# The opening of a fused MetaFormer kernel: corner experts placed ahead of the gates, attention with a second value buffer, and half of the weight splitting moved to POOL

## The chip, the cores and the metric

The kernel runs on one core of a Trainium2 chip. The metric is the device time of one execution in microseconds. Three runs of the kernel before gave 2888.99, 2886.65 and 2889.01 us, median 2888.99 us. The execution whose profile is read here took 2888.1 us, of which 2886.3 us are the span that the profile shows.

## The reference

The input is 16 images of 16x16 positions with 128 channels (4096 tokens). Two layers follow, each with residual sums:

```
x = x + attention(ln_c(x))          # k, v softmax over positions; 64x64 descriptor per image; Wr
t = t + experts(ln_t(t))            # softmax gate, top 2 of 8 experts, each 128 -> 512 gelu -> 128
x = x + grouped_conv(ln_c(x))       # 3x3, 8 groups
t = t + ode(ln_t(t))                # y0 = t[:, 0]; 255 Runge-Kutta steps of a tanh MLP 128-512-512-128
```

The last term is a chain: the solution at position s is step s of an ordinary differential equation whose start is position 0 of every image. Everything is float32; the kernel splits weights and activations of the large products into two float16 halves (high and low) and adds three products.

## The kernel before

**The two parts.** The kernel is a short opening and a long chain. The chain is 255 Runge-Kutta steps; all other work on the 4096 tokens (experts, convolution) is placed beside its steps. The chain needs y0, the final normalised value of position 0 of each image, and that needs the attention of all tokens and then experts and convolution for the four corner positions only. So the opening computes: transposes of x, a first layer norm, attention for four pairs of 512-token tiles, a second layer norm with the gate's logits, the gates, the eight experts for 64 corner tokens, two small norms and the corner of the convolution. Then step 0 starts.

**Order.** All orders are written out by hand, engine by engine; engines meet through counting semaphores. The opening is straight-line code apart from the attention rounds, which are a loop (`Fori`) of three and one written out.

**Attention round i** (`attention_round`, lines 553 to 577 for TensorE, 973 to 985 for ACT, 1159 to 1181 for DVE). TensorE transposes the exponentials of pair i (L557), projects pair i+1 (L549 for keys and queries, L551 for values), forms the descriptors (L565), the output (L571) and the projection Wr (L576), and then waits for the residual of the round. ACT copies TK, copies keys and queries of i+1, copies the output OT, copies the values of i+1 (one buffer V, so only after L571 has read it) and takes the exponentials of i+1 (`exps`, L968 and L970). DVE takes the maxima of the keys of i+1 (L1156), scales the descriptors (L1166), makes the high halves of the fused weights RHU (L1170), takes the maxima of the values, adds the residual to X (L1184), and makes low halves of weights.

**Weight halves.** POOL makes the high halves (L396): four quarters, each of W1 and W2 (1024 columns), RH2 (512), RH3 (128) and CKH (288). DVE makes the low halves of the same, and of the three fused weights (3 x 512 columns), eight instructions a round (`low_halves`, L1189 and L1192). In the last round they stand ahead of the residual.

**Norm, gates, corner experts.** `layer_norm(1)` runs TensorE means (L510) and variances (L516), ACT square, logarithm and exponential, DVE subtraction and product (L1132, L1142), with the gate's logits (L598) beside it. The gates are a chain of 22 DVE instructions (`link`, L1253 to L1275), with one exponential on ACT. TensorE then turns the gates (`turn(0)`, L606), spreads the corner scores (L615), and runs the experts (L625 to L637) with gelu on ACT (L1016) and the split of its result on DVE (L1285, L1287). POOL waits for the gates (`g_ss`) and splits the normalised tokens N into NH (L402) and NL (L405). DVE's small constants (`identities`, `constant`) stand ahead of and between the experts. L1291 closes the experts; the two small norms (`layer_norm` of 64 and 16 columns, L1304 to L1306) give y0 (`rk_y`).

**Step 0** waits on TensorE for the injected base (`rk_ai`), for NL (`n_lo`) and for the gates copied out (`g_sc`). POOL's `base_low(0)` is wanted by TensorE ahead of the last layer of step 0, NH and NL first by the experts beside step 1. SP writes the gates to HBM (L370) and reads them back row by row (L373) into SC, which lies in the memory of the fused weights' source.

## Time and profile before

| what | us |
|---|---|
| three runs, median (lowest, highest) | 2888.99 (2886.65, 2889.01) |
| profiled execution, its own time | 2888.1 |
| its span | 2886.3 |
| TensorE busy, share of the span | 2805.1, 97% |
| DVE busy | 2359.0, 82% |
| ACT busy | 1549.3, 54% |
| POOL busy | 726.9, 25% |

The busy shares are those of the whole span, and 94% of the span is the chain of steps. What is changed lies in the first 168.3 us, so the views to read are the table of busy time by stretch and the timeline of the opening. In a timeline row the first number is the start in us from the span's start, the second the time from start to end of the group, then engine, line, operation, output and inputs with their shape, the count, and in brackets the idle time of that engine before it with what ended it.

### The profile page before, as it was taken

What the parts mean: (1) busy time and instruction counts of PE and PEld (TensorE: products, weight loads), DVE (VectorE), ACT (ScalarE), POOL (GpSimd) and SP (SyncE); (2) the same over time, 40 slices, a digit from 0 to 9 for tenths busy, and PEclk for the clock granted to TensorE, in tenths of its full rate; (3) what the DMA queues carried; (4) which work ended last, traced back from release to release, by engine and by line L of the source; (5) the groups of instructions that cost most, each with busy time, mean ns of one, the idle gap of its engine ahead of it and who ended that gap; (6) DMA issues with size and microseconds to landing.
All of it is one profiled execution on the core that took longest, in us unless ns stands there. A gap on an engine that the chain in (4) does not pass through costs nothing.

```text
span 2886.3 us, 207890 instructions
## 1 busy us (share of the span) xinstructions
PE 2805.1 (97%) x81958; PEld 2402.4 (83%) x81958; DVE 2359.0 (82%) x13272; ACT 1549.3 (54%) x10124; POOL 726.9 (25%) x1346
## 2 busy tenths in 40 slices
PE   7789999999999999999999999999999999999999
PEld 3478888888888888888888887888889999999998
DVE  5778888888888888888888887888888888888887
ACT  6455555555555555555554444444445555555555
POOL 5222332332332332332332000111112222222222
PEclk9789999999999999999999999999999999999999
DMA  3000000000000000000000000000000000000000
GB/s 118 0 12 11 13 12 11 13 12 11 14 12 11 14 12 11 14 12 11 14 11 8 1 0 1 0 0 0 0 17 0 0 0 0 0 0 0 0 0 15
DMA packets 21982, 28.21 MB, mean 10 GB/s; under 512 B 4384, under 2 KB 12896, under 8 KB 21544
## 3 DMA queue, kind: packets, MB, share of 16 engines
q1 hardware_dynamic: 21928, 27.48, 3.1%
q8 instruction: 36, 0.59, 0.1%
q14 instruction: 18, 0.15, 0.0%
HBM read 25.24 MB, written 2.23 MB: 10 GB/s over the span
## 4 chain that ended last, share of the span: by engine, by line
PE 93%; DVE 3%; ACT 2%; issue 1%; DMA 0%; SPq 0%; DVEq 0%; ACTq 0%; POOLq 0%; POOL 0%
PE PSUM L681 22%; PE PSUM L687 21%; PE PSUM L888 17%; PE PSUM L742 12%; PE PSUM L672 5%; PE PSUM L884 4%; PE PSUM L779 1%; DVE PSUM L1395 1%; PE PSUM L844 1%; PE PSUM L849 1%; PE PSUM L708 1%; ACT HA L1072 1%; PE PSUM L712 1%; PE PSUM L749 1%; PE PSUM L510 1%
## 5 line engine op out<-in xcount | busy, mean ns | idle before, releaser
L1395 DVE TENSOR_REDUCE PSUM<-PSUM 128x32 f32<-128x64 f32 x2912 | 624.9, 232 | 96.8 <-PE PSUM L687 51.1
L681 PEld LDWEIGHTS PSUM<-HA,RL 128*128 128x128 f16 x11648 | 396.3, 96 | 205.8 <-ACT HA L1072 196.4
L1073 ACT ACTIVATE PSUM<-PSUM 128x32 f32<-128x32 f32 x2912 | 562.1, 194 | 0.0
L1072 ACT ACTIVATE HA<-PSUM 128x32 f16<-128x32 f32 x1456 | 287.6, 198 | 469.2 <-DVE PSUM L1395 469.1
L1072 ACT ACTIVATE HB<-PSUM 128x32 f16<-128x32 f32 x1456 | 287.9, 199 | 466.0 <-DVE PSUM L1395 466.0
L681 PE MATMUL PSUM<-HA,RL 128*128 128x16 f16 x11648 | 512.1, 170 | 15.3 <-ACT HA L1072 7.6
L681 PE MATMUL PSUM<-HB,RLU 128*128 128x16 f16 x11648 | 511.0, 170 | 3.6
L422 POOL TENSOR_TENSOR G<-G 128x512 f16<-128x512 f32 x256 | 296.6, 1159 | 682.9 <-ACT G L1045 682.9
L687 PE MATMUL PSUM<-HA,RH 128*128 128x32 f16 x11648 | 466.0, 177 | 0.0
L687 PE MATMUL PSUM<-HB,RHU 128*128 128x32 f16 x11648 | 464.8, 177 | 0.0
L681 PEld LDWEIGHTS PSUM<-HB,RLU 128*128 128x128 f16 x11648 | 393.6, 96 | 46.7 <-ACT HB L1072 1.9
L687 PEld LDWEIGHTS PSUM<-HA,RH 128*128 128x128 f16 x11648 | 403.8, 96 | 0.0
L687 PEld LDWEIGHTS PSUM<-HB,RHU 128*128 128x128 f16 x11648 | 402.8, 96 | 0.0
L1405 DVE TENSOR_TENSOR HB<-PSUM,HB 128x32 f16<-128x32 f32 x1456 | 279.9, 192 | 123.0 <-ACT PSUM L1073 114.7
L1405 DVE TENSOR_TENSOR HA<-PSUM,HA 128x32 f16<-128x32 f32 x1456 | 279.9, 192 | 101.1 <-ACT PSUM L1073 86.8
L1045 ACT ACTIVATE G<-PSUM,B1E 128x512 f16<-128x512 f32 (+1 forms) x512 | 353.7, 691 | 0.0
L888 PE MATMUL PSUM<-HB,RLU 128*128 128x32 f16 (+1 forms) x4672 | 338.4, 176 | 0.0
L888 PE MATMUL PSUM<-HA,RL 128*128 128x32 f16 (+1 forms) x4672 | 330.8, 176 | 0.3 <-ACT HA L1107 0.3
L1114 ACT ACTIVATE PSUM<-PSUM 128x16 f32<-128x16 f32 (+1 forms) x1749 | 318.9, 184 | 0.0
L1497 DVE TENSOR_REDUCE PSUM<-PSUM 128x16 f32<-128x32 f32 x1166 | 218.6, 200 | 85.0 <-PE PSUM L888 70.1
L888 PEld LDWEIGHTS PSUM<-HA,RL 128*128 128x128 f16 x4672 | 260.1, 96 | 11.5 <-ACT HA L1107 0.4
L888 PEld LDWEIGHTS PSUM<-HB,RLU 128*128 128x128 f16 x4672 | 260.2, 96 | 11.2
(307 smaller groups left out, 6686.7 us busy)
## 6 DMA issues: line engine op xcount, KB each, us to landing
G<-scores SPq DMA_DIRECT2D x64, 256.0 KB, 3.1
N<-in_x SPq DMA_DIRECT2D x8, 256.0 KB, 4.7
NHL<-in_w SPq DMA_DIRECT2D x1, 2048.0 KB, 10.1
STF<-in_w SPq DMA_DIRECT2D x1, 2048.0 KB, 14.6
out<-W2HL SPq DMA_DIRECT2D x8, 256.0 KB, 2.4
G<-in_r SPq DMA_DIRECT2D x1, 1024.0 KB, 5.3
R1K<-in_r SPq DMA_DIRECT2D x1, 256.0 KB, 2.9
R3F<-in_r SPq DMA_DIRECT2D x1, 256.0 KB, 5.4
```

The costliest lines, as they stand in the source:

```text
L422: g.tensor_tensor(GL[:, m], GF[:, m % 2], GH[:, m], ALU.subtract).then_inc(mo_lo, 1)
L681: mm(out[m // 2][:, 2 * B * (m % 2):2 * B * (m % 2) + B], lo[:, k, m], src[:, k, 0], start=False, stop=False)
L687: t = mm(out[m // 2][:, bass.ts(m % 2, 2 * B)], hi[:, k, m], src[:, k], start=False, stop=(stop and m % 2 == 1 and k == 3))
L742: t = mm(out[:, :], w, v, start=start, stop=stop)
L888: t = mm(repeated(1 - lay, m, B, copies), (lo if kind == "L" else hi)[:, k, m], half, start=False, stop=ends)
L1045: A(GF[:, m % 2] if full else GH[:, m], PS[5 + m % 2][:, :], ACT.Gelu, bias=B1E[:, m:m + 1], scale=1.0 / SCALE_M).then_inc(mo_f if full el ...
L1072: A(hi[:, 2 * h:2 * h + 2, 0], src, ACT.Tanh, scale=1.0 / scale).then_inc(rk_hi, 1)
L1073: A(full, src, ACT.Tanh, scale=1.0 / scale).then_inc(rk_f, 1)
L1114: A(SPLIT_FULL[lay][:, sl], SPLIT_SUM[lay][:, sl], ACT.Tanh, scale=1.0 / scale).then_inc(sp_f[g], 1)
L1395: v.tensor_reduce(bank[:, SUM:SUM + 2 * B].rearrange("p (m b) -> p m b", m=2), bank[:, 0:4 * B].rearrange("p (m c b) -> p m b c", m=2, c=2 ...
L1405: TT(hi[:, sl, 1], full, hi[:, sl, 0], ALU.subtract).then_inc(rk_lo, 1)
L1497: v.tensor_reduce(SPLIT_SUM[lay][:, ms[0]:ms[-1] + 1], PAIRED[lay][g - 1].rearrange("p (m c b) -> p m b c", m=len(ms), c=2), AX.X, ALU.add ...
```

## The change

It changes the order of work in the opening; nothing is left out. The attention rounds are written out for all four pairs. V becomes two buffers, the second in free memory of the norm. The projection of pair i+1 stands ahead of the transposes of pair i, and ACT copies the values of i+1 directly behind the keys. DVE takes the maxima of i+1 ahead of RHU, keeps the low halves of W1 and W2 only, and puts the residual between them. The low halves of the Runge-Kutta, convolution and fused weights (six per quarter) are made by POOL behind the high halves, each with two instructions: a scaled copy in float32 (new buffer SCALED) and a subtraction. Step 0 waits for these 24 (`r_lo`). The corner tokens are split and the experts start directly behind the logits; the gates are made in five parts between the first experts, `turn(0)` stands behind the up-products of the sixth expert and the spreading of scores behind those of the eighth. ACT makes NH, one tile beside each expert. POOL makes NL only behind y0 (`rk_y`), beside step 0; TensorE waits for it ahead of step 1. The constants move into the waits of the small norms.

```diff
-        V = sb("V", [DIM, 2, TILE])
+        V = (sb("V", [DIM, 2, TILE])[:, :, :], SQ4[0:DIM, 2:4])
...
# SP
             sp.wait_ge(w_lo, 4)
+            sp.wait_ge(r_lo, 24)
             sp.dma_start(SC, scores[0:1, :].partition_broadcast(128)).then_inc(sc_in, 16)
...
# POOL
             for q in range(4):
-                for hi, _lo, src, scale in quarter(q):
+                for n, (hi, _lo, src, scale) in enumerate(quarter(q)):
                     t = g.tensor_scalar(hi, src, scale, None, ALU.mult)
-                t.then_inc(w_hi, 1)
+                    if n == 1 or n == 4:
+                        t.then_inc(w_hi, 1)
+            gp.wait_ge(w_hi, 8)
+            for q in range(4):
+                for n, (hi, lo, src, scale) in enumerate(quarter(q)[2:] + fused_quarter(q)):
+                    if n == 3:
+                        gp.wait_ge(u_hi, q + 1)
+                    scaled = SCALED[:, 0:math.prod(src.shape[1:])].rearrange("p (q n) -> p q n", q=1)
+                    g.tensor_scalar(scaled, src, scale, None, ALU.mult).then_inc(r_mul, 1)
+                    gp.wait_ge(r_mul, 6 * q + n + 1)
+                    t = g.tensor_tensor(lo, scaled, hi, ALU.subtract)
+                    t.then_inc(r_lo, 1)
+                    gp.wait_ge(r_lo, 6 * q + n + 1)
             gp.wait_ge(ln_out, 2 * NT)
             gp.wait_ge(w_lo, 4)
-            gp.wait_ge(g_ss, 1)
-            g.tensor_copy(NH, N[:, :]).then_inc(n_hi, 1)
-            gp.wait_ge(n_hi, 1)
+            gp.wait_ge(pm_lo, NE)
+            gp.wait_ge(n_hi, NT)
+            gp.wait_ge(rk_y, 1)
             for t in range(NT):
-                r = g.tensor_tensor(NL[:, bass.ts(t, TILE)], N[:, bass.ts(t, TILE)], NH[:, bass.ts(t, TILE)], ALU.subtract)
-            r.then_inc(n_lo, 1)
+                g.tensor_tensor(NL[:, bass.ts(t, TILE)], N[:, bass.ts(t, TILE)], NH[:, bass.ts(t, TILE)], ALU.subtract).then_inc(n_lo, 1)
...
# TensorE
             def project(i):
+                if i:
+                    pe.wait_ge(at_kq, 2 * i)
...
+                if i:
+                    pe.wait_ge(at_v, 2 * i)
...
-            def attention_round(i, nxt=True):
+            def attention_round(i):
+                if i + 1 < PAIRS:
+                    project(i + 1)
                 for par in range(2):
                     pe.wait_ge(at_exp, 2 * i + par + 1)
...
-                if nxt:
-                    project(i + 1)
                 for par in range(2):
+                    if i:
+                        pe.wait_ge(at_x, 2 * i - 1 + par)
                     pe.wait_ge(at_tk, 2 * i + par + 1)
...
-                pe.wait_ge(at_x, 2 * i + 2)
...
-            pe.wait_ge(g_ss, 1)
-            turn(0)
-            pe.wait_ge(g_stc, 4)
-            for e in range(NE):
-                t = mm(PS[3][:, bass.ts(e, PT)], SELE[:, e], STC[:, :], start=True, stop=True)
-            t.then_inc(pm_s, 1)
+            pe.wait_ge(g_v, 2)
...
                 t.then_inc(pm_h, 1)
+                if e == NE - 3:
+                    pe.wait_ge(g_ss, 1)
+                    turn(0)
+                if e == NE - 1:
+                    pe.wait_ge(g_stc, 4)
+                    for n in range(NE):
+                        t = mm(PS[3][:, bass.ts(n, PT)], SELE[:, n], STC[:, :], start=True, stop=True)
+                    t.then_inc(pm_s, 1)
                 if e:
                     down(e - 1)
...
-            pe.wait_ge(n_lo, 1)
             pe.wait_ge(g_sc, 8)
+            pe.wait_ge(r_lo, 24)
             step(0, True)
+            pe.wait_ge(n_lo, NT)
             moe_round(step, expert, -1, late=False)
...
# ACT
-                if nxt:
+                if i + 1 < PAIRS:
                     copy_kq(i + 1)
+                    copy_v(i + 1)
                 for par in range(2):
                     act.wait_ge(at_o, 2 * i + par + 1)
                     nc.scalar.copy(OT[:, par], PA[par][0:DIM, :]).then_inc(at_ot, 1)
-                if nxt:
-                    copy_v(i + 1)
+                if i + 1 < PAIRS:
                     exps(i + 1)
...
                 t.then_inc(pm_g, 1)
+                nc.scalar.copy(NH[:, bass.ts(e, TILE)], N[:, bass.ts(e, TILE)]).then_inc(n_hi, 1)
+                if e == NE - 2:
+                    corner_scores()
...
             act.wait_ge(w_lo, 4)
+            act.wait_ge(r_lo, 24)
             step(0, True)
...
# DVE
-            def attention_round(i, nxt=True):
+            def attention_round(i):
+                reciprocals(i)
...
                     t.then_inc(at_gds, 1)
+                if i + 1 < PAIRS:
+                    maxima(i + 1, 0)
+                    maxima(i + 1, 1)
                 for hi, lo, src, scale in fused_quarter(i):
                     t = TS(hi, src, scale, None, ALU.mult)
                 t.then_inc(u_hi, 1)
+                dve.wait_ge(w_hi, 2 * i + 1)
+                low_half(quarter(i)[0])
+                residual(i)
+                low_half(quarter(i)[1]).then_inc(w_lo, 1)
...
             link(TT(GA[:, :, :], LOGITS, wide(0), ALU.subtract))
             v.tensor_copy(corners(PNH[:, :]), corner(N[:, :])).then_inc(pm_n, 1)
             dve.wait_ge(pm_n, 1)
             TT(corners(PNL[:, :]), corner(N[:, :]), corners(PNH[:, :]), ALU.subtract).then_inc(pm_n, 1)
-            identities()
+            biases()
...
+            gates(0)
             for e in range(NE):
...
                 TT(PGL[:, e % 2], PGF[:, e % 2], PGH[:, e % 2], ALU.subtract).then_inc(pm_lo, 1)
-                if 3 <= e < 7:
-                    constant(e - 3)
+                gates(e + 1)
+            identities()
...
                 TT(D[:, 0, 0:width], src[:, :], PA[0][:, 0:width], ALU.subtract).then_inc(ln_dev, 1)
+                constant(2 * n)
```

The five parts of the gates hold 5, 4, 4, 4 and 3 of the 20 instructions from L1256 to L1275, in their old order.

## Rows read from the trace of the kernel before

**Rows 1.** Stretch, length; busy us (count) of PE, PEld, DVE, ACT, POOL; PE clock; DMA
```profile
38.20:98.80 60.60, 44.53 (x169) 23.45 (x169) 45.34 (x96) 30.49 (x84) 41.82 (x19) 0.79 0.00 0
98.80:123.60 24.80, 24.40 (x104) 15.18 (x104) 11.13 (x18) 13.99 (x24) 0.00 (x0) 0.91 0.00 1
123.60:155.90 32.30, 15.34 (x227) 12.44 (x228) 25.49 (x60) 12.84 (x43) 13.05 (x9) 0.63 0.01 1
...
143.41:144.69 1.28, 1.27 (x24) 1.27 (x24) 1.25 (x2) 0.00 (x0) 1.28 (x2) 0.50 0.06 13
...
168.30:2886.30 2718.00, 2685.99 (x81342) 2332.24 (x81342) 2258.51 (x13063) 1461.08 (x9914) 665.03 (x1311) 0.99 0.02 7
```

**Rows 2.** Timeline, TensorE: the matmul groups of an attention round, and the last round's start
```profile
29.75 1.96 PE L549 MATMUL PSUM<-N,WKQ 128*128 128x512 f32 x4
...
61.66 1.09 PE L565 MATMUL PSUM<-SQ 128*64 128x64 f32 x16
...
62.92 1.99 PE L571 MATMUL PSUM<-V,GD 64*128 64x256 f32 x8 [0.17 <-DVE GD L1166]
...
64.75 1.95 PE L576 MATMUL PSUM<-D,WR 64*128 64x512 f32 x4
...
84.94 0.66 PE L557 MATMUL PSUM<-ID,D 128*128 128x128 f32 x4 [2.33 <-ACT V L970]
```

**Rows 3.** Timeline, ACT: first exponential of one pair, and the TK copy behind the last
```profile
66.90 0.51 ACT L968 ACTIVATE D<-D,NM 64x256 f32<-64x256 f32 x1 [0.22 <-DVE NM L1156]
...
70.85 0.56 ACT L977 COPY SQ<-PSUM 128x512 f32<-128x512 f32 x1
```

**Rows 4.** Timeline, DVE: one attention round
```profile
63.25 1.08 DVE L1170 TENSOR_SCALAR RHU<-G  x3
...
66.14 1.27 DVE L1156 TENSOR_REDUCE NM<-V 64x2 f32<-64x512 f32 x2 [1.81 <-ACT V L960]
...
67.34 1.39 DVE L1184 SCALAR_TENSOR_TENSOR X<-PSUM,BR,X 128x512 f32 x2
...
68.65 1.21 DVE L1189 SCALAR_TENSOR_TENSOR W1HL<-NHL,W1HL  x1
```

**Rows 5.** Timeline, TensorE: the means of the first and of the second layer norm
```profile
12.33 3.70 PE L510 MATMUL PSUM<-X,ONES 128*128 128x512 f32 x8 [0.76 <-ACT X L947]
...
98.78 6.02 PE L510 MATMUL PSUM<-X,ONES 128*128 128x512 f32 x8 [2.95 <-DVE X L1184]
```

**Rows 6.** Timeline, POOL: high halves, the last of them, and the eight NL subtractions
```profile
38.17 1.49 POOL L396 TENSOR_SCALAR RH<-G 128x512 f16<-128x512 f32 x1
...
68.41 8.20 POOL L396 TENSOR_SCALAR W2HL<-STF 128x1024 f16<-128x1024 f32 x1
...
78.72 1.79 POOL L396 TENSOR_SCALAR CKH<-CK 128x288 f16<-128x288 f32 x1
...
137.44 9.39 POOL L405 TENSOR_TENSOR NHL<-N,NHL 128x512 f16<-128x512 f32 x8
```

**Rows 7.** Timeline, DVE: instructions beside a busy POOL, and a cast beside an idle one
```profile
38.20 0.59 DVE L1198 TENSOR_TENSOR RP<-SE 64x2 f32<-64x2 f32 x1 [3.21 <-ACT V L970]
...
143.28 1.24 DVE L1285 CAST SQ<-D 128x256 f16<-128x256 f32 x1
...
150.01 0.29 DVE L1285 CAST SQ<-D 128x256 f16<-128x256 f32 x1 [0.33 <-PE PSUM L627]
```

**Rows 8.** Timeline, DVE, TensorE and ACT: first and last gate, turn, spreading of scores, gelu
```profile
125.02 0.42 DVE L1256 TENSOR_REDUCE GR<-GP 128x32 f32<-128x256 f32 x1 [0.56 <-ACT GP L998]
...
133.11 0.42 DVE L1275 TENSOR_TENSOR GP<-GP,GR 128x256 f32<-128x256 f32 x1
...
133.59 3.58 PE L606 MATMUL PSUM<-ID,GP 128*8 128x128 f32 x16 [10.04 <-DVE GP L1275]
...
137.41 2.08 PE L615 MATMUL PSUM<-STC,SELE 8*128 8x64 f32 x16 [0.25 <-ACT STC L1005]
...
150.64 0.93 ACT L1016 ACTIVATE D<-PSUM,B 128x64 f32<-128x64 f32 x4 [0.72 <-PE PSUM L637]
```

More of the change, by code:

```diff
@@ L17 @@
+import math
 from contextlib import ExitStack
@@ L219, in build @@
         ck_zero, consts, w_hi, u_hi, w_lo = (sem(k) for k in ("ck_zero", "consts", "w_hi", "u_hi", "w_lo"))
+        r_mul, r_lo = sem("r_mul"), sem("r_lo")
         x_tr, x_c = sem("x_tr"), sem("x_c")
@@ L583, in _ @@
             pe.wait_ge(w13_out, MC)
-            with pe.Fori(0, PAIRS - 1) as i:
+            for i in range(PAIRS):
                 attention_round(i)
-            attention_round(PAIRS - 1, False)
+            pe.wait_ge(at_x, NT)
             def logits(place):
@@ L992, in _ @@
             exps(0)
-            with act.Fori(0, PAIRS - 1) as i:
+            for i in range(PAIRS):
                 attention_round(i)
-            attention_round(PAIRS - 1, False)
             layer_norm(1, 1)
@@ L1001, in turned, with corner_scores @@
                 nc.scalar.copy(dst, PS[4 + k][0:NE, :].rearrange("e (b n) -> e b n", b=4)).then_inc(g_sc, 1)
[L1003 to L1008 removed]
+            def corner_scores():
+                for k in range(4):
+                    act.wait_ge(g_st, k + 1)
+                    nc.scalar.copy(STC[:, bass.ts(k, PT // 4)].rearrange("e (b y x) -> e b y x", b=4, y=2),
+                                   PS[4 + k][0:NE, :].rearrange("e (b y x) -> e b y x", b=4, x=HW)[:, :, 0:2, 0:2]).then_inc(g_stc, 1)
             nc.scalar.preload_act_table_set("gelu_and_others")
+            act.wait_ge(w_lo, 4)
             for e in range(NE):
@@ L1017, in _ @@
                 t.then_inc(pm_g, 1)
+                nc.scalar.copy(NH[:, bass.ts(e, TILE)], N[:, bass.ts(e, TILE)]).then_inc(n_hi, 1)
+                if e == NE - 2:
+                    corner_scores()
+            for k in range(4):
+                turned(k, 0)
             nc.scalar.preload_act_table_set("natural_log_exp_and_others")
@@ L1025, in _ @@
                 A(SD[:, 0, 0:width], SD[:, 0, 0:width], ACT.Exp, scale=-0.5).then_inc(ln_sd, 1)
-            for k in range(4):
-                act.wait_ge(g_st, 4 + k + 1)
-                turned(k, 1)
+                if n == 0:
+                    for k in range(4):
+                        act.wait_ge(g_st, 4 + k + 1)
+                        turned(k, 1)
             nc.scalar.preload_act_table_set("gelu_and_others")
@@ L1171, in attention_round @@
                 t.then_inc(u_hi, 1)
-                if nxt:
-                    maxima(i + 1, 1)
-                    residual(i)
-                    low_halves(i)
-                    reciprocals(i + 1)
-                else:
-                    low_halves(i)
-                    residual(i)
+                dve.wait_ge(w_hi, 2 * i + 1)
+                low_half(quarter(i)[0])
+                residual(i)
+                low_half(quarter(i)[1]).then_inc(w_lo, 1)
             def residual(i):
@@ L1184, in residual, with low_half @@
                     STT(X[:, tile(i, par)], PB[par][:, :], BR[:, :], X[:, tile(i, par)], ALU.add, ALU.add).then_inc(at_x, 1)
-            def low_halves(i):
-                dve.wait_ge(w_hi, i + 1)
-                for hi, lo, src, scale in quarter(i):
-                    STT(lo, src, scale, hi, ALU.mult, ALU.subtract)
-                dve.wait_ge(u_hi, i + 1)
-                for hi, lo, src, scale in fused_quarter(i):
-                    t = STT(lo, src, scale, hi, ALU.mult, ALU.subtract)
-                t.then_inc(w_lo, 1)
+            def low_half(half):
+                hi, lo, src, scale = half
+                return STT(lo, src, scale, hi, ALU.mult, ALU.subtract)
             def reciprocals(i):
@@ L1204, in _ @@
             maxima(0, 1)
-            reciprocals(0)
             dve.wait_ge(w13_out, MC)
-            with dve.Fori(0, PAIRS - 1) as i:
+            for i in range(PAIRS):
                 attention_round(i)
-            attention_round(PAIRS - 1, False)
             dve.wait_ge(at_x, NT)
```

77 lines of the change are left out of this document (39 added, 38 removed).

## The prediction

> **What bounds the kernel now.** I read the busy time by stretch first [rows 1], then the timeline of the opening engine by engine. The chain of 255 steps begins at 168.3 us and takes 2718.0 us, 10.7 a step; the change touches nothing in it, so I price the 168.3 us ahead of it. Four stretches matter: attention (38.2 to 98.8), second norm with logits (to 123.6), gates and corner experts (to 155.9), small norms (12.4 us, to 168.3). In attention no engine is busy for more than 45.3 of 60.6 us, and TensorE's clock is granted at 0.79: engines wait for each other in turn. In the third stretch TensorE is busy for 15.3 of 32.3 us, and its first turn stands behind 10.04 us of idling on the last gate [rows 8]. Only the norm is full (TensorE 24.4 of 24.8 us). So there is room in two stretches, and little in the others.
>
> **Attention.** The last round's transposes start at 84.94 [rows 2], the first at 38.2: 15.6 us a round. The change takes the projection from behind the transposes, the values' copy and maxima from behind the output, and six low halves a round from DVE. What is left for TensorE at full clock is two transposes (0.66 each), two projections (1.96 each), 1.09, 1.99 and 1.95: 10.3 us [rows 2]. DVE keeps RHU 1.08, four maxima 2.54, residual 1.39 and two low halves 2.42: 7.4 [rows 4], which leaves 2.9 for the small scalings and for waits on POOL. So TensorE sets the round at 10.3, and as it then hardly idles I take the full clock; that is the floor, 10.3 / 0.79 = 13.0 the ceiling. The last interval holds no projection; there ACT decides: transposes 0.7, six copies of about 0.56, the two key copies and two value copies among them longer, and half of the exponentials make about 8.
>
> The first transposes wait for exponentials and now also for a projection. A pair's exponentials take 70.85 - 66.90 = 3.95 [rows 3] and begin once W13 is copied out, at 38.2 less half of that: 36.2. Only then can the projection run ahead (3.9), so the first transposes move from 38.2 to 40.1, a loss of 1.9. Then 10.3 + 10.3 + 8 lead to 68.7. From there the last round took 98.78 - 84.94 = 13.8 [rows 2, 5]. Now it is: second half of the exponentials 2.0, transposes 0.7, TK copy 0.6, half of the products 0.5, scaling 0.5, half of the output 1.0, OT copy 0.6, half of Wr 1.0, residual 1.4, and 0.4 for POOL; RHU and one low half lie beside the others. That is 8.7: the norm starts at 77.4, not 98.78, **21.4 gained**.
>
> The added waits cost nothing by this. The projection waits for copies made a round earlier, the products for the last residual. DVE's `w_hi` waits for POOL's W1 and W2 of the round's quarter; behind it stand the residual and, through it, the next products. POOL ends all quarters at 80.51 now, with 5.2 us lost on each of two W2 instructions that stood still (8.20, against 3.0 at 1.49 for 512 columns) [rows 6], so without such stalls W2 of the last quarter is there by about 72, and is wanted at about 74. If it is not, each us late is a us lost.
>
> **Norm.** Its means took 6.02 against 3.70 in the first norm [rows 5]: they followed 2.95 us of idling and the clock was low; that idling goes, so 2.3 less. But POOL is now busy beside it. A cast beside POOL's subtractions took 1.24, beside an idle POOL 0.29: it waited 0.95, where one such subtraction takes 9.39 / 8 = 1.17 [rows 6, 7]. Eight multiplies with two SBUF inputs may each wait that long, 0 to 7.6 us; TensorE's pace hides most, I take 1.0. **1.3 gained**; the logits end at 100.9.
>
> **Gates and experts.** Now 32.3 us [rows 1]. After: 0.9 for two links and 1.2 for corner halves and biases (estimates from 0.42 and 0.29); five gates; then for each of four experts a cast of 0.29 and a subtraction of 0.42 with 15 gates between them. The 20 gates ran from 125.02 to 133.53 [rows 8], 0.43 each: 0.9 + 1.2 + 8.5 + 2.8 = 13.4 to the last gate. ACT's table load, gelu (0.93) and NH copies (about 0.56, as the TK copy [rows 3]) lie beside these, since 1.5 an expert on ACT is under 2.4 on DVE. POOL's locks add 0 to 24 (some 25 exposed instructions at 0.95); POOL's scalings and subtractions leave the lock free about half the time and DVE fills part of it, I take 4.0. Behind the last gate stand the turn 3.58, two products of 0.64 (24 matmuls in 1.27 at half clock [rows 1]), gelu and NH 1.5, four score copies 0.6, spreading 2.08, two products of 0.64: 10.3 at half clock, 6.2 at full; I take 8.2 [rows 8]. Sum 25.6: **6.7 gained**; L1291 starts at 126.5. Constants and the second turn's copies go into waits of the small norms; one that sticks out costs up to 0.6; I take 0.4, so 12.8 there. The first injection comes at 139.3, **29.0 earlier**.
>
> **POOL.** Its high halves end between 66.9 (80.51 less two stalls of 5.2 and three RHU runs of 1.08) and 77.4 (that plus 3.5 of contending DVE work in each of three rounds); I take 72. Then each quarter has 2464 columns to scale and to subtract: 7.2 at 1.49 per 512, and 5.6 at 1.17 [rows 6]. A scaled copy to float32 is not in the trace: bounds 0.9 per 512 and 2.0, the nearest row kept. With 48 hand-overs of 0.1 (estimate) that is 56 us. DVE's contending work in that stretch adds 0 to 16 (half of the norm's 11.13, gates, casts); half is 8. The last low half lands at 136, 3 us ahead of the injection, so the new wait of TensorE, ACT and SP costs nothing; if it lands later, all three wait. NL (9.39) now follows y0 beside step 0, where DVE reads mostly PSUM; behind it on POOL stand the copy of y0 and `base_low(0)`, wanted 7/8 into a step of 10.7, at 9.4: 0 to 1.0, I take 0.
>
> **Sum.** 21.4 + 1.3 + 6.7 - 0.4 = 29.0 off the profiled execution's own 2888.1, which is 0.9 under the median of the runs: **2859 us**.
>
> **A rule against it.** The POOL instruction at 38.17 ran until 39.66; DVE's two-operand instruction beside it ended at 38.79 [rows 6, 7]: the wait was shorter than the instruction. The Trainium skill, "SBUF — State Buffer", section "Who interferes with whom", says that a DVE instruction with two SBUF inputs or in a two-port mode and a POOL instruction exclude each other for the whole instruction; the trace agrees that they do, not on how long. By it the sum would be that of rival 3.
>
> **Rivals.** (1) *POOL ends last* (0.17). High halves at 77.4 and 16 us of blocking put the last low half at 149; step 0 waits with all else ready: 19 gained, 2869. For it: W2 stood still twice [rows 6]. Against: DVE's runs are shorter now. (2) *The half clock stays in attention* (0.12). Two rounds of 13.0, one of 9 and slow means lose 8.7: 2868. For it: 0.79 now [rows 1]. Against: TensorE's work now fills the exponentials' time. (3) *Exclusion for the whole instruction* (0.13). POOL is busy until about 130; from 103 on one DVE instruction passes per POOL instruction of 1.2, 22 of 25 in that time, so the last gate comes near 132 rather than 118, and 2 are lost in the norm: 13 gained, 2875. (4) *Better* (0.12): no lock waits (5.4) and full clock behind the gates (2.0): 2852. (5) *Slower* (0.04): POOL's pairs of scaling and subtraction starve. 24 pairs from 72 on: at (168.3 - 72) / 24 = 4.0 us a pair step 0 starts as late as now, while the rows give 56 / 24 = 2.3; at 4.5 it starts at 180: 2900. (6) *Nothing is moved in the end* (0.03): what attention gives comes back as the wait for `r_lo`, 2888.
>
> **How the numbers follow.** The forecast has 0.39. The range takes in rivals 1 to 4 up to their outer parts and leaves out (5) and (6): 2848 to 2876. A measurement of this kernel can tell about 0.2%, 5.8 us, from no change: faster 0.93 (forecast and rivals 1 to 4), same 0.03, slower 0.04.
>
> **What would show it.** Right: transposes of successive rounds 10 to 11 us apart, then 8, at a granted clock near 1; the norm starting near 77; the last gate near 118 with casts of the first experts between the gates; the last low half on POOL a few us ahead of the injection; step 0 and all later steps as long as before. Wrong: TensorE idle ahead of step 0 with POOL as its releaser (1); a clock under 0.85 in attention (2); gates or casts that take 1 us or more (3); `w_hi` as a releaser of DVE ahead of a residual.

## The result, and the profile after

Four executions of the changed kernel took 2866.97, 2864.96, 2862.34 and 2871.75 us, median 2865.97; the kernel before took 2888.61 beside them (four executions). The ratio is 0.9925, 95% interval 0.9913 to 0.9938: 0.75% faster. Two later sets gave 0.9929 (0.9913 to 0.9946) and 0.9925 (0.9913 to 0.9938). The forecast was 2859 us with a range of 2848 to 2876. The execution whose profile follows is the first of the four: 2866.97 us, span 2864.7. Of the 29.0 us that were forecast, this span shows 21.6.

The table of busy time by stretch, of the kernel after. The columns are those of [rows 1]; the stretches are attention (from the first transposes), second norm with logits, gates and experts, small norms, and the steps.
```profile
41.80:78.60 36.80, 32.02 (x161) 18.08 (x160) 30.35 (x68) 27.35 (x76) 36.17 (x18) 1.00 0.00 1
78.60:101.40 22.80, 22.47 (x104) 14.51 (x104) 13.64 (x18) 14.00 (x24) 21.26 (x19) 0.99 0.00 1
101.40:130.80 29.40, 16.39 (x226) 14.18 (x226) 22.58 (x47) 15.73 (x51) 27.35 (x25) 0.56 0.00 1
130.80:146.60 15.80, 9.43 (x41) 7.49 (x40) 10.53 (x25) 5.36 (x12) 9.22 (x9) 0.50 0.12 26
146.60:2864.70 2718.10, 2684.84 (x81342) 2330.39 (x81342) 2257.22 (x13063) 1462.62 (x9913) 670.55 (x1316) 0.99 0.02 7
```
Read the lengths first. Attention starts 3.6 us later than before and ends 20.2 earlier. The norm takes 22.8 instead of 24.8, gates and experts 29.4 instead of 32.3, the small norms 15.8 instead of 12.4. The steps take what they took (2718.1 against 2718.0). So the four experts that now stand among the gates, the split on POOL and the moved constants together gain nothing: the last two stretches before step 0 took 44.7 us and take 45.2. In this execution attention and norm are the whole gain; in the two other profiles of this kernel (below) the last two stretches took 41.8 and 41.2, about 3 us less than before. Then read PEclk: 1.00 in attention, as forecast, and 0.56 and 0.50 in the two stretches where TensorE is busy for 16.4 of 29.4 and 9.4 of 15.8 us.

The timeline of TensorE after (columns as in [rows 2]): the projection that now stands ahead of the first transposes, the transposes of the four rounds, and the norm's first means.
```profile
36.48 3.52 PE L564 MATMUL PSUM<-N,WKQ 128*128 128x512 f32 x4 [2.73 <-issue]
...
41.79 1.09 PE L576 MATMUL PSUM<-ID,D 128*128 128x128 f32 x8
...
52.05 1.09 PE L576 MATMUL PSUM<-ID,D 128*128 128x128 f32 x8
...
62.32 1.09 PE L576 MATMUL PSUM<-ID,D 128*128 128x128 f32 x8
...
69.67 0.66 PE L576 MATMUL PSUM<-ID,D 128*128 128x128 f32 x4 [0.78 <-ACT SQ L992]
...
78.63 3.70 PE L523 MATMUL PSUM<-X,ONES 128*128 128x512 f32 x8 [1.22 <-DVE X L1210]
```
The rounds are 10.26, 10.27 and 7.35 us long, against 15.6 in [rows 2], and the means take 3.70 instead of 6.02 [rows 5].

The same view for VectorE among the gates, and for POOL beside it. L1288 and L1287 are gates, L1314 and L1316 are the cast and the subtraction of an expert's gelu, L1278 is the subtraction of the corner tokens, L1307 the last gate, L1320 the sum that closes the experts.
```profile
102.59 1.22 DVE L1278 TENSOR_TENSOR PNL<-N,PNH 128x64 f16<-128x64 f32 x1
...
104.97 0.42 DVE L1286 TENSOR_TENSOR GP<-GP,GR 128x256 f32<-128x256 f32 x1
105.42 0.42 DVE L1287 TENSOR_REDUCE GR<-GP 128x32 f32<-128x256 f32 x1
105.88 0.95 DVE L1288 TENSOR_TENSOR GA<-GP,GR 128x256 f32<-128x256 f32 x1
106.86 0.58 DVE L1314 CAST SQ<-D 128x256 f16<-128x256 f32 x1
107.48 0.43 DVE L1316 TENSOR_TENSOR SQ<-D,SQ 128x256 f16<-128x256 f32 x1
...
119.72 0.43 DVE L1307 TENSOR_TENSOR GP<-GP,GR 128x256 f32<-128x256 f32 x1
...
130.84 0.69 DVE L1320 TENSOR_TENSOR D<-PSUM,B 128x512 f32<-128x512 f32 x1 [1.95 <-PE PSUM L640]
```
```profile
102.58 1.15 POOL L411 TENSOR_TENSOR RLU<-SCALED,RHU 128x512 f16<-128x512 f32 x1
103.82 1.49 POOL L409 TENSOR_SCALAR SCALED<-G 128x512 f32<-128x512 f32 x1
105.40 1.15 POOL L411 TENSOR_TENSOR RLU<-SCALED,RHU 128x512 f16<-128x512 f32 x1
106.64 1.54 POOL L409 TENSOR_SCALAR SCALED<-G 128x512 f32<-128x512 f32 x1
...
134.46 1.15 POOL L411 TENSOR_TENSOR RLU<-SCALED,RHU 128x512 f16<-128x512 f32 x1
...
141.94 8.94 POOL L421 TENSOR_TENSOR NHL<-N,NHL 128x512 f16<-128x512 f32 x8 [6.33 <-DVE Y L1336]
```
A gate takes 0.42, a cast 0.29 and L1278 0.23 when nothing is in the way. L1278 stands for 1.22, L1288 for 0.95, the cast for 0.58: each began while a POOL instruction was in its first part. Take the usual length off the end of each row, and what is left is where the wait ended: 1.0 us behind the start of POOL's subtraction (1.15 long) for the first two, 0.5 us behind the start of its scaling (1.5 long) for the cast. Such a wait beside POOL is what the prediction and the expectations call its lock. The reduction L1287, which began 0.02 us behind POOL's subtraction, did not wait. Twelve such waits between logits and last gate add up to 5.9 us, each taken as what a row has over the usual length of its kind. POOL's last low half ends at 135.6, 11 us ahead of the first injection, so the new wait of TensorE, ACT and SP costs nothing.

The end of the opening, VectorE and TensorE: last constants and the base state beside POOL's NL subtractions, then the injection.
```profile
142.11 1.03 DVE L1254 CAST CI<-CW 128x64 f16<-128x64 f32 x1
143.18 1.11 DVE L1256 TENSOR_TENSOR CI<-CW,CI 128x64 f16<-128x64 f32 x1
...
144.58 0.79 DVE L1350 CAST AI<-US 128x64 f16<-128x64 f32 x1
145.40 1.10 DVE L1352 TENSOR_TENSOR AI<-US,AI 128x64 f16<-128x64 f32 x1
```
```profile
146.56 0.29 PE L832 MATMUL PSUM<-AI,IDU 128*128 128x64 f16 x2 [2.85 <-DVE AI L1352]
```
Casts and subtractions of 64 columns take 0.8 to 1.1 us here; in the stretch ahead of y0, where POOL is idle, the same lines take 0.20 and 0.23. From y0 to the injection 4.79 us pass, before it were 2.75.

### The profile page after: what moved, and what is told of

It reads as the page before. It is cut to its first block, busy times and chain, and to the rows that moved or that the text cites. A ratio compares the mean times of both kernels' runs of the same rounds, so it can differ in the third digit from the quotient of the medians.

```text
span 2864.7 us, 207841 instructions
## 1 busy us (share of the span) xinstructions
PE 2798.6 (98%) x81958; PEld 2399.7 (84%) x81958; DVE 2348.9 (82%) x13248; ACT 1553.5 (54%) x10132; POOL 774.5 (27%) x1393
## 4 chain that ended last, share of the span: by engine, by line
PE 93%; DVE 3%; ACT 2%; issue 1%; DMA 0%; SPq 0%; POOLq 0%; DVEq 0%; POOL 0%; ACTq 0%
PE PSUM L702 23%; PE PSUM L708 21%; PE PSUM L910 17%; PE PSUM L763 12%; PE PSUM L693 5%; PE PSUM L906 4%; DVE PSUM L1427 1%; PE PSUM L800 1%; PE PSUM L866 1%; PE PSUM L871 1%; PE PSUM L729 1%; ACT HA L1100 1%; PE PSUM L733 1%; PE PSUM L770 1%; PE PSUM L523 0%
## 5 line engine op out<-in xcount | busy, mean ns | idle before, releaser
L1437 DVE TENSOR_TENSOR HA<-PSUM,HA 128x32 f16<-128x32 f32 x1456 | 279.6, 192 | 101.4 <-ACT PSUM L1101 82.2
```

The source lines that it names most:

```text
L1437: TT(hi[:, sl, 1], full, hi[:, sl, 0], ALU.subtract).then_inc(rk_lo, 1)
```

## The experiments

The comparison is made in stretches, because executions differ (below). Each row is one profiled execution; all times are starts or ends of rows of its timeline, in us. The logits are taken to end where the first gate starts.

| kernel | norm starts | norm and logits | logits to last gate | to final sum | to y0 | to injection | injection at |
|---|---|---|---|---|---|---|---|
| before | 98.8 | 24.8 | 10.0 | other order | other order | 2.75 | 168.3 |
| after | 78.6 | 22.8 | 18.7 | 10.7 | 10.9 | 4.79 | 146.6 |
| after_again | 80.7 | 22.8 | 18.2 | 8.1 | 10.7 | 4.80 | 145.2 |
| after_third | 81.5 | 26.8 | 18.2 | 8.1 | 10.0 | 4.79 | 149.4 |
| no_lows | 82.7 | 26.9 | 12.8 | 9.0 | 10.2 | 4.81 | 146.5 |
| lows_dve | 89.2 | 25.0 | 12.8 | 8.8 | 9.7 | 4.79 | 150.3 |
| gates_first | 83.1 | 25.4 | 13.1 | 22.1 | 9.8 | 4.79 | 158.2 |
| nl_late | 82.8 | 24.5 | 19.0 | 10.5 | 9.8 | 2.82 | 149.5 |
| project_behind | 88.7 | 22.5 | 20.0 | 10.4 | 9.6 | 4.79 | 156.0 |
| one_value | 81.8 | 24.2 | 18.7 | 10.4 | 9.8 | 4.79 | 149.8 |
| hold_last | 80.4 | 25.5 | 18.9 | 9.4 | 10.2 | 4.80 | 149.3 |
| filler | 81.2 | 23.0 | 18.0 | 7.3 | 10.2 | 4.78 | 144.5 |
| split | 79.2 | 25.2 | 12.8 | 10.7 | 9.6 | 2.82 | 140.4 |
| split_two | 81.7 | 25.7 | 12.9 | 10.7 | 9.9 | 2.82 | 143.5 |

Times of kernels are compared by their ratio to the kernel before on the same chip; 0.001 is 2.9 us. The changed kernel's three sets have a mean of 0.9926, and differences to it below are from this mean; sets were taken on different chips.

**Why executions differ.** after_again and after_third are the changed kernel once more, unedited.

> The changed kernel itself once more, as the yardstick of this set and to see how far its executions spread. Theory A (the gain is attention's and the norm's, the corner part gives back what its new order wins) and every rival: about 2866 us, first injection near 146.6 us.

> The changed kernel once more, beside the two others on one chip. From its two earlier sets: ratio to before 0.9925 to 0.993, executions some 5 to 9 us apart. If the spread is made by TensorE's clock in the last attention round, the profile shows the norm's start between 78.6 and 83 us and the logits' end between 101.4 and 109 us, and behind the first injection a chain that is as long per stage as in the other profiles within 0.2%.

Fourteen executions of it in three sets lie between 2860.9 and 2872.9 us, 9.4, 5.4 and 11.3 us apart within a set, where the kernel before has 2.4, 2.8 and 4.0. The three profiles have the same length of their first three attention rounds (10.3, 10.3 and 7.3) and part in the last one. The table by stretch of the first, then of the third:
```profile
68.00:72.00 4.00, 1.91 (x10) 0.84 (x9) 4.00 (x7) 4.00 (x17) 3.94 (x3) 1.00 0.01 4
72.00:76.00 4.00, 3.84 (x29) 2.84 (x27) 3.52 (x12) 1.55 (x4) 3.77 (x4) 1.00 0.00 0
76.00:80.00 4.00, 2.78 (x7) 0.97 (x6) 3.84 (x6) 0.24 (x1) 3.91 (x2) 1.00 0.00 0
80.00:84.00 4.00, 4.00 (x11) 1.82 (x10) 2.61 (x4) 2.03 (x4) 3.66 (x5) 1.00 0.00 0
```
```profile
68.00:72.00 4.00, 2.13 (x12) 1.57 (x13) 3.76 (x8) 3.26 (x13) 3.87 (x4) 0.74 0.00 0
72.00:76.00 4.00, 4.00 (x21) 3.42 (x20) 2.81 (x7) 0.68 (x2) 3.75 (x4) 0.50 0.00 0
76.00:80.00 4.00, 4.00 (x7) 1.76 (x6) 2.16 (x3) 0.74 (x2) 3.66 (x5) 0.50 0.00 0
80.00:84.00 4.00, 3.16 (x4) 1.17 (x4) 3.03 (x3) 0.00 (x0) 3.83 (x3) 0.50 0.00 0
```
In both TensorE is busy for about 2 of 4 us from 68 to 72, where the last round has no projection to run ahead. In one the clock stays at its full level, in the other it falls to the lower one until 84 to 88 (in the second of the three for some 4 us): the descriptors, output and means take twice as long, norm and logits end at 108.3 instead of 101.4. So rival 2 of the prediction is true of the last round in some executions and false in others. The time of an execution goes with its mean granted clock, which is on record for every run. In the set of after_third the three executions at 0.987 took 2861.6 to 2863.9 us, the two at 0.984 took 2868.5 and 2869.5, the one at 0.981 took 2872.9; in the first set 0.987 goes with 2862.3 and 0.982 with 2871.8. A mean that is lower by 0.003 is some 17 us more at the lower level in an execution of 2866 us (an estimate: 0.003 x 2866 / 0.5), and here it goes with 5 to 8 us. So most of the spread is time at the lower clock; where it lies in the executions that were not profiled is not seen.

A second, smaller part is even over the whole program: 181 stages of the chain, between the first and the last of 182 rows of one POOL line, took 1963.75 us in the profile of after and 1960.06 in that of after_again, 0.19% less, and less in every stretch of eight stages. The two come from different sets, and the kernel before was 0.13% shorter beside after_again (2884.96 against 2888.61), so the chip can be a part of it. It is not all: on one chip the same stages took 1963.38 in after_third and 1960.34 in one_value, which has the same code there.
```profile
153.77 0.31 POOL L427 TENSOR_TENSOR AI<-VS,AI 128x64 f16<-128x64 f32 x1 [2.62 <-DVE VS L1451]
...
2117.52 0.31 POOL L427 TENSOR_TENSOR AI<-VS,AI 128x64 f16<-128x64 f32 x1 [7.68 <-DVE VS L1451]
```
```profile
152.36 0.30 POOL L427 TENSOR_TENSOR AI<-VS,AI 128x64 f16<-128x64 f32 x1 [2.61 <-DVE VS L1451]
...
2112.42 0.30 POOL L427 TENSOR_TENSOR AI<-VS,AI 128x64 f16<-128x64 f32 x1 [7.68 <-DVE VS L1451]
```

hold_last gives TensorE something to do there:
```diff
+                if i + 1 == PAIRS:
+                    pe.wait_ge(at_kq, 2 * PAIRS)
                 for par in range(2):
+                    if i + 1 == PAIRS:
+                        mm(PS[4 + par][:, :], WKQ[:, :], N[:, tile(i, par)], start=True, stop=True)
                     pe.wait_ge(at_exp, 2 * i + par + 1)
```


> The changed kernel with one projection of the last pair done once more ahead of each of the two transposes of the last round, with nobody reading it, where TensorE otherwise stands idle for 0.8 and 1.3 us. Of five profiles of this order of work three show the lower granted clock from 72 to 84 us and a norm that starts at 82.7 to 83.1 and logits that end at 107.3 to 109.6; two show it at or near full and 78.6 and 80.7, 101.4 and 103.4. Theory A (the executions differ by whether TensorE's clock falls in the last round): the clock stays full from 40 to 100, the norm starts at 77.5 to 79, logits end by 102; the median is 3 to 5 us below the changed kernel's and the runs lie within 4 us of one another. Rival B (the spread is made in the steps of the ODE behind the opening): the opening is the same or 1 us later, the median the same within 2 us and the runs spread by 6 us and more. Rival C (the fall comes whatever TensorE does there): clock at half in 72 to 84 as often as before, time 0 to 2 us longer.

Ratio 0.9929 (0.9915 to 0.9943), executions 4.3 us apart (2865.7 to 2870.0). The clock held until 76 and fell from 76 to 84 instead; norm and logits took 25.5. Theory A falls in its numbers (norm at 80.4, logits to 105.9), the spread of 6 us and more of B is not there, and C describes the profile best: two matmuls did not hold the clock. What makes it fall in some executions and not in others stays open.

**The lower halves on POOL.** no_lows leaves the 24 scaled copies and subtractions out and sets those low halves to zero, so the Runge-Kutta, convolution and fused weights have high halves only.
```diff
+            for a in (RL2[:].rearrange("p e m n -> p (e m n)"), RL3[:].rearrange("p m n -> p (m n)"), CKL[:, :],
+                      RLU[:].rearrange("p c e m n -> p (c e m n)")):
+                g.memset(a, 0.0).then_inc(r_lo, 1)
...
-            for q in range(4):
-                for n, (hi, lo, src, scale) in enumerate(quarter(q)[2:] + fused_quarter(q)):
...
```


> Leaves out the 24 scalings and subtractions on POOL: the low halves of the Runge-Kutta, convolution and fused weights are set to zero at the start, so three of the products beside them are with zeros. Theory A: POOL's lock stands in DVE's way in the norm and the gates; last gate 13.5 us after the logits instead of 18.8, the norm 1 us shorter, attention 1 us shorter, injection near 139, total 7 us less. Rival (the half clock of TensorE alone explains the missed 7 us): last gate as late as before within 1 us, injection at 145 or later.

Ratio 0.9896 (0.9880 to 0.9913), 8.7 us below the changed kernel's 0.9926. Logits to last gate: 12.8 us. Its first and last gate on VectorE:
```profile
109.59 0.42 DVE L1271 TENSOR_REDUCE GR<-PSUM 128x32 f32<-128x256 f32 x1 [2.88 <-PE PSUM L610]
...
122.00 0.43 DVE L1304 TENSOR_TENSOR GP<-GP,GR 128x256 f32<-128x256 f32 x1
```
The same instructions take 5.9 us less with POOL idle: the waits are shown, and the forecast's 13.4 for this stretch without them was close. The two other terms of theory A, a norm that is 1 us shorter and an injection near 139, are not seen: the profile is the slowest of the four executions (2864.6 of 2853.2 to 2864.6), its clock is at the lower level from 72 to 88, norm and logits took 26.9 and the injection came at 146.5.

lows_dve takes POOL's loop of 24 out and gives the same work back to VectorE, in the rounds:
```diff
                 low_half(quarter(i)[1]).then_inc(w_lo, 1)
+                dve.wait_ge(w_hi, 2 * i + 2)
+                dve.wait_ge(u_hi, i + 1)
+                for half in quarter(i)[2:] + fused_quarter(i):
+                    low_half(half).then_inc(r_lo, 1)
```


> The changed kernel, but the 24 low halves that POOL makes are made by VectorE again, six at the end of each attention round. Theory A (the offload buys VectorE's time in attention and pays it back as lock waits beside POOL later): about 3.1 us of work come back per round on VectorE, which has some 2 us idle in a round of 10.3, so rounds of about 11.4 and a norm that starts 5 to 6 us later; against it no POOL work stands beside the gates, logits to last gate takes about 13 us instead of 18.8, and the first injection comes out within 3 us of the changed kernel's; time within 3 us of its median. Rival B (the offload is where the change's gain lies): 8 us slower or more. Rival C (the offload as a whole loses): 4 us faster or more.

Ratio 0.9939 (0.9926 to 0.9953), 3.8 us above the changed kernel, with overlapping intervals; the norm starts 8 to 11 us later than in its profiles, and the gates take 12.8. The offload buys some 8 us in attention and pays 6 back at the gates. That is theory A, 0.8 us beyond its bound, with the gates as it has them; its even rounds of 11.4 are not there. They took 10.3, 17.2 and 7.3: in the second VectorE's reciprocals stand behind the low halves, TensorE waits for the scaled descriptors, and its clock falls (0.50 from 60 to 68).

**The order of gates and experts.** gates_first makes the gates, the turn and the spreading ahead of the experts, as before, and leaves the rest.
```diff
+            for part in range(5):
+                gates(part)
...
-                gates(e + 1)
```


> Undoes the new order of gates and corner experts alone: all gates, the turn and the spreading of scores stand ahead of the corner split and the experts again; attention, POOL's low halves, NH on ACT and NL stay as changed. Theory A: the order is worth something here: last gate about 13.5 us after the logits, then turn 3.6, spreading 2.5 and eight experts of 2 us, so L1320's sum starts 36 to 38 us after the logits instead of 29.4, total 6 to 8 us more. Rival: the new order is worth nothing beside a busy POOL, total within 2 us.

Ratio 0.9953 (0.9936 to 0.9969), 7.8 us above the changed kernel. The gates alone take 13.1 us beside POOL (10.0 before), and everything from the logits to the final sum 35.2 us instead of the 26 to 29 of the three profiles of the changed kernel. So the new order is worth 6 to 9 us here, and POOL's low halves cost a good part of it back: with none on POOL (no_lows) the same stretch took 21.9.

**NL.** nl_late lets POOL's eight subtractions wait for the base state's second half (`rk_ai`) instead of y0 (`rk_y`).
```diff
-            gp.wait_ge(rk_y, 1)
+            gp.wait_ge(rk_ai, 1)
```


> POOL makes NL only once the base of step 0 is done (rk_ai) and no longer from y0 (rk_y) on; the same work. Theory A: between y0 and the injection DVE's casts and subtractions wait for POOL's lock, 4.8 us in the changed kernel against 2.75 in the one before; without NL beside them the injection comes 2.0 us earlier (144.5), step 0 keeps its length, the total falls by about 2 us. Rival: NL then ends too late for the base of step 1 (base_low), step 0 grows by what is won, the total stays.

Ratio 0.9914 (0.9898 to 0.9931), 3.5 us below the changed kernel with overlapping intervals; the stretch itself is plain, 2.82 us from y0 to the injection:
```profile
148.95 0.19 DVE L1350 CAST AI<-US 128x64 f16<-128x64 f32 x1
149.18 0.23 DVE L1352 TENSOR_TENSOR AI<-US,AI 128x64 f16<-128x64 f32 x1
```
0.19 and 0.23 in place of 0.79 and 1.10. The injection came at 149.5 and not at the forecast 144.5: the profile is the slowest of the four executions (2869.3 of 2857.9 to 2869.3), and its clock is at the lower level from 72 to 84. The rival falls: POOL's rows for the bases of steps 0 and 1 (L427) start 9.3 and 18.7 us behind the injection, against 7.2 and 19.2 in after, so the later NL holds up the first and step 0 does not grow by it.

**What carries attention.** project_behind puts the projections behind the transposes again; one_value has one V buffer and copies the values behind the heads' output again.
```diff
-                if i + 1 < PAIRS:
-                    project(i + 1)
...
                     t.then_inc(at_tr, 1)
+                if i + 1 < PAIRS:
+                    project(i + 1)
```


> The changed kernel with the projections of the next pair behind the transposes again, all else as changed. Theory A (the projection ahead fills TensorE's wait for the exponentials and keeps its clock): gaps of 2 to 3 us ahead of the transposes, granted clock at its lower level in a part of each round, rounds of about 12 instead of 10.3, the norm starts 6 to 8 us later and the time is 6 to 8 us longer. Rival B (the round is set by ScalarE and VectorE, the order on TensorE only fills idle time): rounds of 10.3 to 10.8, time within 2 us of the changed kernel's.

Ratio 0.9970 (0.9960 to 0.9980): 12.7 us above the changed kernel, more than theory A expected, and rival B falls. Rounds of 13.4, 13.6 and 13.6; the gaps ahead of the transposes are 0.9 and 1.3 us, not 2 to 3. The chain of waits of one round (start, length, what):
```profile
53.71 1.11 PE PSUM L574 x4
54.82 2.91 PE PSUM L564 x4
57.73 1.86 PE PSUM L568 x4
...
61.38 2.38 DVE NM L1185 x4
...
67.33 1.11 PE PSUM L574 x4
```
From one round's transposes the chain runs through the projection and the maxima of the next pair to its exponentials and its transposes: the projection lies in it in full length. With the projection ahead this branch has a whole round.

```diff
-        V = (sb("V", [DIM, 2, TILE])[:, :, :], SQ4[0:DIM, 2:4])
+        V = (sb("V", [DIM, 2, TILE])[:, :, :],) * 2
...
-                    copy_v(i + 1)
                 for par in range(2):
                     act.wait_ge(at_o, 2 * i + par + 1)
...
                 if i + 1 < PAIRS:
+                    copy_v(i + 1)
                     exps(i + 1)
```


> The changed kernel with one value buffer instead of two: the copies of the next pair's values stand behind the copies of the heads' output again, as they did before the change; the projections stay ahead of the transposes. Theory A (the second buffer is what lets ScalarE start the next exponentials a wait earlier; project_behind alone cost 3.4 us per round): the four value copies and the maxima of the values come behind the heads' output, rounds of 12 to 13.5 instead of 10.3, the norm starts 5 to 9 us later, ratio to before 0.995 to 0.997. Rival B (the order of the projections carries the whole gain, the buffer none): rounds of 10.3 to 10.8, ratio 0.992 to 0.994.

Ratio 0.9949 (0.9936 to 0.9962), 6.6 us above the changed kernel, at the expected time; but the rounds of its profile are 10.2, 10.8 and 9.4, not 12 to 13.5. Only the last one shows the wait (TensorE idle ahead of the last transposes):
```profile
71.87 1.12 PE L576 MATMUL PSUM<-ID,D 128*128 128x128 f32 x4 [2.34 <-ACT V L992]
```
That profile is the shortest of its five executions (2866.4 of 2866.4 to 2875.9); where the others lose up to 9 us more no trace shows. The intervals overlap, and at the mean clock of 0.984 three of its executions (2866.4 to 2872.2) lie about where the changed kernel's two lie on that chip (2868.5, 2869.5); what it lacks are executions at 0.987. So that the second buffer is worth some 6.6 us is likely and not shown clear of the spread; the wait is seen in the last round only.

**TensorE's clock beside the gates.** filler adds 30 matmuls that nobody reads.
```diff
+            fill(5)
             pe.wait_ge(g_v, 2)
...
+                if e <= 4:
+                    fill(5)
```


> The changed kernel with 30 matmuls of 512 columns that nobody reads, five ahead of the first expert and five behind each of the first five, to keep TensorE busy between the logits and the turn of the gates. Theory A (what the corner part lost against the forecast is in part TensorE's lower clock there): the granted clock between 102 and 131 us is full for most of it, the 16 transposes of the turn take 1.8 us instead of 3.6, the final sum stands 7 to 8.5 us behind the last gate instead of 10.7; time 2 to 4 us below the changed kernel's. Rival B (the clock falls all the same, or the matmuls stand in the experts' way): the same sum 10 us or more behind the last gate, time 0 to 4 us longer.

```profile
108.00:112.00 4.00, 2.03 (x39) 1.32 (x36) 3.83 (x7) 1.80 (x6) 3.66 (x5) 1.00 0.00 0
...
116.00:120.00 4.00, 1.95 (x29) 1.25 (x29) 3.79 (x8) 1.87 (x9) 3.74 (x4) 1.00 0.02 4
...
124.00:128.00 4.00, 3.12 (x62) 2.87 (x61) 2.52 (x4) 3.07 (x15) 3.57 (x6) 1.00 0.01 2
...
```
```profile
122.29 1.91 PE L625 MATMUL PSUM<-ID,GP 128*8 128x128 f32 x16
```
The clock is full there (0.50 from 104 to 124 in the changed kernel), the turn takes 1.91 instead of 3.60, and 7.25 us pass from the last gate to the final sum, as theory A has it. Yet the ratio is 0.9934 (0.9920 to 0.9947), no better than without. Its profile, one of the faster of its executions (2865.6 of 2862.9 to 2872.9), has its injection at 144.5, ahead of all three profiles of the changed kernel. Both executions at 0.989 took 2862.9 and 2865.6, the three at 0.986 took 2869.6 to 2872.9: the slower ones had more time at the lower clock, and where was not seen. As a means to save time it is not shown.

**Half of the low halves on POOL.** split leaves POOL the first 12 low halves, done near the end of the logits, and gives VectorE the other 12 where it waits; NL as in nl_late. split_two places VectorE's 12 differently.
```diff
-            for q in range(4):
+            for q in range(2):
                 for n, (hi, lo, src, scale) in enumerate(quarter(q)[2:] + fused_quarter(q)):
...
                     TT(N[:, bass.ts(t, TILE)], D4[:, t % 4], SQ4[:, t % 4], ALU.mult).then_inc(ln_out, 1)
+                    if p and t in IN_NORM:
+                        lows(IN_NORM[t])
...
                 gates(e + 1)
+                if e in IN_CORNER:
+                    lows(IN_CORNER[e])
```


> The changed kernel with POOL making only the first 12 of the 24 low halves (done about 3 us behind the logits instead of 34), VectorE the other 12 where it waits anyway: one behind each of the first six tiles of the second norm, five behind expert 5, one behind expert 7; and POOL's subtraction for the low half of the norm's output waiting for the base state's second half instead of y0. Theory A (POOL's lows cost the corner part about 6 us of waits among the gates, the subtraction 2 us at its end, and neither has to): logits to last gate 12.8 to 14 us instead of 18 to 19, the norm no more than 1 us longer than its 22.8 at full clock, y0 to injection 2.8 instead of 4.8; the first injection 6 to 9 us earlier at the same clock in the last attention round; ratio to before 0.9895 to 0.991, against 0.9927 of the changed kernel. Rival B (the 12 halves stand in VectorE's way as long as the waits did): ratio 0.992 or more.

Ratio 0.9905 (0.9891 to 0.9920), median 2859.92; its executions (2858.0 to 2861.9) lie below all but one of the changed kernel's on that chip (2861.6 to 2872.9), though the intervals of the ratios overlap. At the same mean clock of 0.987 it took 2858.0 against 2861.6 to 2863.9, so the spread of the clock is not the whole difference. Of this NL is a part: the edit holds that of nl_late too. The injection comes at 140.4. Gates 12.8 and 2.82 to the injection as forecast, the norm 2.4 too long.

> As the split kernel, with VectorE's 12 low halves placed by what that kernel's trace shows: its norm took 25.2 us from the means to the logits' end instead of 22.8, since each half stands between two tiles and some wait beside POOL; ahead of the first tile's product VectorE waits 3.1 us. So four go there, the others behind expert 5 (five), 6 (one) and 7 (two). Theory A (only placement was wrong): the norm 22.5 to 23.5 us at full clock, the stretch from the last gate to the final sum no more than 0.7 us longer than the 10.7 of the split kernel, the first injection at 138 to 139 instead of 140.4, ratio to before 0.989 to 0.9902. Rival B (the halves cost VectorE's time wherever they stand): the gain in the norm comes back behind the experts, ratio 0.9903 to 0.992.

Ratio 0.9906 (0.9889 to 0.9922): no different from split, with the injection at 143.5 and not at 138 to 139 and the norm at 25.7, not 22.5 to 23.5. Its profile has the low clock in the last round, so its injection (143.5) is to be set against after_third's (149.4), 5.9 earlier in the same case; the norm took 25.7 against 26.8 there. Which placement is better is not told apart.

## Why the prediction was right, and where its steps were not

**Attention (21.4 forecast, 20.2 came).** Rounds 10.3, 10.3 and 8 against 10.26, 10.27 and 7.35; clock 1.00; the first transposes at 41.8 instead of 40.1, the norm at 78.6 instead of 77.4. The small error is in part luck: the first transposes were 1.7 late and the way from the last ones to the norm 0.3 long, and rounds that are 0.7 shorter took some of it back. The late start is a matter of the clock: the first projection took 3.52 for its keys and queries (granted 0.57 from 36 to 40) and 1.96 in after_third (1.00 there), where the prediction took the 1.96 of the full clock. The steps hold: the projection ahead had to be there (12.7 us); for the second buffer (6.6) and the offload (3.8, net of the gates) the medians say so, with overlapping intervals. What failed is "as it then hardly idles I take the full clock" for the last round, which has no projection: of the three profiles of the changed kernel one keeps the clock there, and in the others the norm starts up to 2.9 us later and ends up to 6.9 later.

**Norm (1.3; 2.0).** Means at 3.70 as reckoned, 2.3 less; of the 1.0 taken for waits beside POOL 0.3 came.

**Gates and experts (6.7; 2.9).** Three terms. The 13.4 to the last gate without waits was right (12.8). "I take 4.0" for POOL's locks was low: 5.9. And "6.2 at full; I take 8.2", the middle between two levels of the clock, came in two of the three profiles of the changed kernel (8.1) and not in the one that is read here (10.7); with the clock held (filler) it is 7.3.

**Small norms (-0.4; -3.4).** This step failed. "one that sticks out costs up to 0.6" priced the moved constants; not priced was that NL, moved from beside the experts to behind y0, falls on four of the last instructions ahead of the injection, which have two operands in SBUF or are casts (two of them belong to the last of the moved constants). The prediction asked what NL would hold up on POOL (nothing, as it came) and not whom it would lock out on VectorE: 2.0 us, shown by nl_late. The rest goes mostly with the lower clock of this execution: from the final sum to y0 it took 10.9, the other kernels 9.6 to 10.7 (before: 9.7), and the eight convolution products in it took 1.88 us here and 1.05 in split, by their chains of waits.

**POOL.** High halves end at 73.8 (72 forecast), the last low half at 135.6 (136), the scaled copy takes 1.49 per 512 columns, the row that was kept as nearest. Ahead of the injection by 11 us instead of 3 since the injection is later. Rival 1 is out.

**The rule.** A DVE instruction waited for a POOL scaling during its first 0.5 of 1.5 us only; L1286, at 104.97 beside the scaling that began at 103.82, took its usual 0.42, and L1316, at 107.48 beside the one that began at 106.64, its usual 0.43. The Trainium skill, "SBUF — State Buffer", section "Who interferes with whom", has the exclusion last for the whole instruction, by which, in the prediction's working, rival 3 would have come: 2875 us. The measurement decides: for POOL's subtractions the rule nearly holds (1.0 of 1.15), for its scalings it does not. The same section says that a reduction never contends on trn2; the trace agrees (L1287, 0.42 beside a subtraction).

In sum 7.4 us of the 29.0 are missing in the profiled execution: 1.2 in attention, 3.8 at gates and experts, 3.0 at the small norms, and the norm gave 0.7 more; the steps took 0.1 more. Attention and norm gave 22.2 of the 22.7 that were forecast for them. What stands behind them was forecast to give 6.3 and gave -0.5 in this execution, about 3 in the two other profiles, and there the lower clock in the last round cost 2 to 7 us of the rest. So the mechanism was right where the gain is large and mis-sized behind it; the median lies 7 us above the forecast, and the range held because it took in rivals of 2868 to 2875 us.

## What to carry to other kernels

Work moved to POOL is not free for VectorE's two-operand and cast instructions beside it: price it where it will run, not where it is wanted, and keep it away from chains of short dependent instructions (gates, the last state ahead of a start). Put a branch that feeds the next round (projection, copies, maxima) ahead of the wait of this round, with a buffer of its own; undoing the one cost 13 us, undoing the other some 7 by the medians. And read the granted clock stretch by stretch over more than one execution: one stretch of one program ran at the full level in one execution and at the lower in another (norm and logits 22.8 and 26.8 us), and a sum that takes a middle value says nothing about either.

## What was not expected of the hardware

One POOL instruction shuts out VectorE's casts and two-operand instructions for a part of its length that depends on its kind: 0.5 of 1.5 us for a scaling of 512 columns, 1.0 of 1.15 for a subtraction. TensorE's clock stayed full from 108 to 132 us with TensorE busy for 2.0 to 3.7 of each 4 us (filler), and in the last attention round, behind some 2 of 4 us, it fell in two of three executions of one program and stayed in the third. And two profiled executions of one program differed by 0.19%, evenly over 181 stages, and on one chip two of programs that are the same there by 0.15%.
